# A two-layer AdaLN block (linear attention, RWKV and two FP4 feed-forwards) on one core: residual adds by an adding DMA, norm sums taken by ScalarE, a channel-mix key of half the matmuls, merged quantization halves, and feed-forward weights made ready inside the first turns

## What is computed

```python
h = layernorm(x) * (1 + ca) + sa
x = x + ga * attention(h)                      # x1, x3
h = layernorm(x) * (1 + cb) + sb
x = x + gb * ffn(h)                            # x2, x4
# ffn: gate, up = fp4(h) @ fp4(w_gate).T, fp4(h) @ fp4(w_up).T      (128 -> 352)
#      out = fp4(silu(gate) * up) @ fp4(w_down).T                   (352 -> 128)
# fp4(v): blocks of 16 along the last axis, scale = max|block| / 6, values rounded to 8 magnitudes
# layer 0: q, k, v, beta, mix = projections of h, rope on q and k, phi = elu + 1
#      K[t] = K[t-1]*beta + phi_k ; S[t] = S[t-1]*beta + phi_k v    (two decays m per head)
#      y = sum_m mix_m * (phi_q S) / (phi_q K) ; z = h + y @ Wout.T + bout ; layernorm(z) * g + b
# layer 1: RWKV: xn = layernorm(x) ; k, v, r = (xn mixed with the token before) @ weights
#      x = x + wkv(k, v) * sigmoid(r) @ w_output
#      xn2 = layernorm(x) ; key = (xn2*mix + shift(xn2)*(1-mix)) @ f_w_key    (128 -> 512)
#      x + sigmoid(receptance) * (relu(key)**2 @ f_w_value)
```

## Time and profile before

| what | value |
|---|---|
| median of 3 runs | 1495.9 us (1495.53 to 1497.5) |
| the profiled execution: its own time | 1494.11 us |
| its span, from the first to the last instruction | 1492.3 us |
| mean granted clock of TensorE, as a share of 2.4 GHz | 0.946 |
| busy: PE, DVE, ACT, POOL | 1290.4, 1202.6, 959.7, 191.6 us |
| x loaded, out stored | 16 DMAs each, 256 KB |

### The profile page before, as it was taken

How to read it: one execution, slowest core, us unless ns; L and a number is a source line. 1 busy time by engine, 2 the same in 40 slices (tenths; PEclk the granted TensorE clock), 3 DMA queues, 4 the chain that set the end, 5 groups by cost and what they waited for, 6 DMA issues and landing times.

```text
span 1492.3 us, 19655 instructions
## 1 busy us (share of the span) xinstructions
PE 1290.4 (86%) x5770; PEld 803.0 (54%) x5770; DVE 1202.6 (81%) x2423; ACT 959.7 (64%) x2145; POOL 191.6 (13%) x238
## 2 busy tenths in 40 slices
PE   1466898898989898989989898989989898989775
PEld 1233355555656565555656565655656565656453
DVE  6558677789898898979888898979888898986554
ACT  1434565758586767768585767768585767766664
POOL 1000202011111102021111102011110102020000
PEclk9968899999999999999999999999999999999897
DMA  3000000000000000000000000000000000000000
GB/s 117 0 8 1 7 1 1 8 1 8 8 8 8 8 1 15 1 16 0 7 7 7 9 0 14 0 15 0 7 7 7 9 0 14 0 7 1 8 7 14
DMA packets 21333, 13.45 MB, mean 9 GB/s; under 512 B 1396, under 2 KB 20472, under 8 KB 21240
## 3 DMA queue, kind: packets, MB, share of 16 engines
q1 hardware_dynamic: 12792, 8.29, 1.9%
q10 hardware_dynamic: 8448, 4.20, 1.0%
HBM read 8.28 MB, written 4.19 MB: 8 GB/s over the span
## 4 chain that ended last, share of the span: by engine, by line
PE 68%; ACT 11%; DVE 9%; issue 8%; POOL 2%; DMA 0%; ACTq 0%; DVEq 0%; SPq 0%; POOLq 0%
PE ps L1059 8%; PE ps L1155 6%; PE ps L852 4%; PE ps L964 4%; PE ps L1255 4%; PE ps L872 4%; PE ps L887 4%; PE ps L1246 3%; PE ps L1122 3%; PE ps L1247 3%; PE ps L960 2%; PE ps L926 2%; PE ps L898 2%; PE ps L1192 2%; PE ps L939 2%
## 5 line engine op out<-in xcount | busy, mean ns | idle before, releaser
L1059 PE MATMUL ps<-wguT,hqcol 128*128 128x352 f32 x512 | 174.5, 476 | 3.9 <-issue 3.9
L1500 DVE TENSOR_TENSOR_SCAN state<-beta,outer 128x512 f32<-128x512 f32 x128 | 149.2, 1207 | 0.0
L1059 PEld LDWEIGHTS ps<-wguT,hqcol 128*128 128x128 f32 x512 | 94.5, 197 | 63.0 <-issue 25.7
L401 POOL TENSOR_TENSOR rstd_of_a<-var_of_a,minus_half 128x4 f32<-128x4 f32 x32 | 39.1, 1222 | 625.0 <-DVE var_of_a L1460 625.0
L1360 DVE SCALAR_TENSOR_TENSOR hid<-hmag,hid 128x704 f32<-128x704 f32 x128 | 113.0, 883 | 2.0 <-ACT hmag L652 0.4
L1155 PE MATMUL ps<-hidcol,wdT 128*128 128x256 f32 (+1 forms) x384 | 94.8, 390 | 3.9 <-DVE outer L1491 2.0
L1577 DVE TENSOR_TENSOR hid<-th,ps 128x352 f32<-128x352 f32 x128 | 64.6, 515 | 26.9 <-ACT th L639 18.3
L1155 PEld LDWEIGHTS ps<-hidcol,wdT 128*128 128x128 f32 (+1 forms) x384 | 70.4, 193 | 26.7 <-DVE outer L1491 10.3
L639 ACT ACTIVATE th<-ps 128x352 f32<-128x352 f32 x128 | 59.6, 467 | 37.6 <-PE ps L1059 34.5
L1526 DVE TENSOR_TENSOR state<-state,qk 128x1024 f32<-128x1024 f32 x64 | 76.1, 1209 | 0.0
L660 ACT ACTIVATE hidcol<-ps 128x512 f32<-128x512 f32 x64 | 38.2, 597 | 57.7 <-PE ps L1122 57.0
(11 more groups left out here) (232 smaller groups left out, 3417.0 us busy)
## 6 DMA issues: line engine op xcount, KB each, us to landing
xin<-in_x SPq DMA_DIRECT2D x16, 256.0 KB, 2.8
out<-x ACTq DMA_DIRECT2D x16, 256.0 KB, 2.3
const<-in_const SPq DMA_DIRECT2D x1, 848.0 KB, 6.1
state<-in_wmod SPq DMA_DIRECT2D x1, 768.0 KB, 4.7
outer<-in_w_gate_up SPq DMA_DIRECT2D x2, 128.0 KB, 6.1
wqk<-in_wqk SPq DMA_DIRECT2D x1, 256.0 KB
key_mixed<-in_fw_key SPq DMA_DIRECT2D x1, 256.0 KB
fw_val<-in_fw_val SPq DMA_DIRECT2D x1, 256.0 KB
```

Source lines behind the costliest of these rows:

```text
L1059: t_.matmul(bank(f"f{l}_{'gu'[g]}{t}")[:, 0:I_FF], hqcol[l][:, t * P:(t + 1) * P], wguT[:, l, g, :], start=True, stop=True).then_inc(s_gu[ ...
L1500: return v.tensor_tensor_scan(state[:, m, c, :], beta[:, m, :], src, 0.0, ALU.mult, ALU.add)
```

## The change

**Residual adds.** x is loaded straight into the rows `xa`, where the sums x1 and x2 stay; x3 and x4 are in `xb`. For x1, x3 and x4 TensorE only transposes the gated term to rows (`rows_from`), ScalarE copies it to SBUF, and a DMA issued by GpSimd adds it to the rows in place (`accum_op=ALU.add`). Each of these DMAs stands behind a tiny `tensor_tensor` into `pool_scrap`. x2 stays on TensorE.

**Norm sums.** f0, a1 and f1 lose `bn_stats` and `bn_aggr`. ScalarE's copy out of PSUM is cut in four tiles that accumulate their row sums (`rows_out`), VectorE makes the mean with one small instruction (`mean_f0` and its like; for f0 and f1 it is the old rows' mean plus the added term's), ScalarE squares the deviations from SBUF in four tiles (`spread_squares`, after the DMA has landed), and GpSimd needs three small instructions (`power_of_spread`) where it had two.

**Mixed key.** ScalarE (`c5x`) and VectorE (`c5k`) mix the channel mix's input once, into `xk`, and four matmuls do the key where eight did.

**z matmuls.** The two halves over m are summed in PSUM (`a_n`), so `a6` has one set over `ycol`; `bout` is added by ScalarE to a copy of the columns (`a1b`, `hcolb`). `a5y` copies `a_n` out on ScalarE and `a5q` multiplies on VectorE.

**Merged halves.** `b4`, `b4q` and three steps of `c4` work on whole tiles: 1408 values a row in place of twice 704.

**Cut of the turns.** The turn is cut at another place: the ends of `a4` and `a5` of pair n - 1 stand at the top of turn n, `b1` of layer 1 is at n - 3 throughout, and the store is at n - 4.

**Weights.** The early loads are reordered (x of pair 0 third), and the quantization of the feed-forward weights is spread in 18 pieces a layer over VectorE's turns 0 and 1 (`weight_blocks`), their transposes too (`turn_weights`); `late_weights` makes the rest ready in turn 0.

The diff, cut to its core:

```diff
+        hmag = [hidcol[l].rearrange("p c t -> p (c t)")[:, 0:NT * I_FF] for l in range(2)]
...
+        def at_start(step, pair, *more):
+
+            if isinstance(pair, int) and pair == 0:
+                step(*more)
...
+            sp.dma_start(cT[:, :, :], a["cT"]).then_inc(s_cond, 16)
+            sp.dma_start(wmod[:, :, :], a["wmod"].rearrange("l p n -> p l n")).then_inc(s_wmod, 16)
+            sp.dma_start(of_pair(xa, 0), x_v[0, :, :, :]).then_inc(s_x[0], 16)
+            sp.dma_start(const[:, :], a["const"]).then_inc(s_const, 16)
+            for dst, src in ((wvT, "wv"), (wbmT, "wbm"), (vec[:, :], "vec"), (bbeta[:, :], "bbeta"), (bmix[:, 0:2], "bmix"),
+                             (wqk[:, :, :], "wqk"), (woutT[:, :], "wout")):
+                sp.dma_start(dst, a[src]).then_inc(s_load, 16)
+            sp.dma_start(bout[:, :], a["bout"].rearrange("o h -> h o")).then_inc(s_load, 16)
...
+            def power_of_spread(ln, i):
+                pool.wait_ge(s_squares[ln], i + 1)
+                before(pool, s_norm[ln], i, NT)
+                g.tensor_tensor(var[ln][:, :], squares[ln][:, :], eps_sum[:, :], ALU.add).then_inc(s_shift[ln], 1)
+                after(pool, s_shift[ln], i, 3, 1)
                 g.tensor_tensor(rstd[ln][:, :], var[ln][:, :], minus_half[:, :], ALU.pow).then_inc(s_shift[ln], 1)
-                after(pool, s_shift[ln], i, 2, 1)
-                g.tensor_tensor(shift[ln][:, :], negm[ln][:, :], rstd[ln][:, :], ALU.mult).then_inc(s_shift[ln], 1)
...
+            def add_x1(i):
+                pool.wait_ge(s_urow, i + 1)
+                g.tensor_tensor(pool_scrap[:, 0, :], minus_half[:, :], eps_tile[:, :], ALU.mult)
+                g.dma_start(of_pair(xa, i), urow[:, :, :], accum_op=ALU.add).then_inc(s_x1, 16)
...
             def body(n):
+                do(power_f0, n - 2)
+                do(power_c1, n - 3)
+                do(add_x4, n - 4)
+                do(add_x3, n - 3)
                 do(power_f1, n - 3)
-                do(power_f0, n - 1)
+                do(power_a1, n - 2)
+                do(power_b1, n - 2)
                 do(power_a0, n)
-                do(power_c1, n - 2)
-                do(power_a1, n - 1)
-                do(power_b1, n - 1)
-                do(power_z0, n)
+                do(power_z0, n - 1)
+                do(add_x1, n - 1)
             turns(pool, body)
 
...
+            def spread_squares(ln, i, rows, spare):
+                act.wait_ge(s_mean[ln], i + 1)
+                for t in range(NT):
+                    at = (i % 2) * NT + t
+                    ins = s.activation(spare[:, t, :], rows[:, at, :], ACT.Square, bias=negm[ln][:, at:at + 1],
+                                       accum_out=squares[ln][:, t:t + 1])
+                ins.then_inc(s_squares[ln], 1)
+
+            def rows_out(ln, i, name, dst, done):
+                before(act, s_mean[ln], i)
+                for t in range(NT):
+                    ins = s.activation(dst[:, t, :], tiles_of(name)(t), ACT.Copy, accum_out=sums[ln][:, t:t + 1])
+                ins.then_inc(done, 1)
+
+            def b1v(l, i):
+                before(act, s_fqT[l], i)
+                if l == 0:
+                    act.wait_ge(s_x1, 16 * i + 16)
+                else:
+                    act.wait_ge(s_x3, 16 * i + 16)
+                spread_squares(f"f{l}", i, (xa, xb)[l], hq[l])
+
+            def c1v(j):
...
-            def a5(i, q):
-                after(act, s_share_mm, i, SEQ, q + 1)
-                s.activation(share_c[:, :, q * T:(q + 1) * T], bank(f"a_s{q}").rearrange("p (m t) -> p m t", m=M), ACT.Copy)\
-                    .then_inc(s_share_c, 1)
+            def a5y(i):
+                after(act, s_num, i, 2 * M)
+                before(act, s_z, i)
+                s.activation(ycol[:, :], bank("a_n"), ACT.Copy).then_inc(s_yc, 1)
...
+            def c5x(j):
+                act.wait_ge(s_xs[1], j + 1)
+                before(act, s_fk_mm, j, 4)
+                s.activation(xk.rearrange("p (s t) -> p s t", s=SEQ), xs[1][:, :, 0:T], ACT.Identity, scale=omix[:, 3:4]).then_inc(s_xkp, 1)
...
-                    last = t_.matmul(bank(f"a_n{m}")[c * NH:(c + 1) * NH, :], cst("sel_num"), state[:, m, c, :], start=True, stop=True,
-                                     tile_position=(0, c * NH))
+                    last = t_.matmul(bank("a_n")[c * NH:(c + 1) * NH, :], cst("sel_num"), state[:, m, c, :], start=(m == 0),
+                                     stop=(m == M - 1), tile_position=(0, c * NH))
                 last.then_inc(s_num, 1)
...
-                t_.matmul(bank("a_z"), ones_row[:, :], bout.rearrange("p t h -> p (t h)"), start=True, stop=False)
...
-                    t_.matmul(dst, hcol[0][:, t * P:(t + 1) * P], center, start=False, stop=False)
-                    t_.matmul(dst, ycol[:, 0, t * P:(t + 1) * P], woutT[:, :], start=False, stop=False)
-                    last = t_.matmul(dst, ycol[:, 1, t * P:(t + 1) * P], woutT[:, :], start=False, stop=(t == NT - 1))
+                    t_.matmul(dst, hcolb[:, t * P:(t + 1) * P], center, start=True, stop=False)
+                    last = t_.matmul(dst, ycol[:, t * P:(t + 1) * P], woutT[:, :], start=False, stop=True)
...
-            def a8x(i):
-                pe.wait_ge(s_x, 16 * i + 16)
-                freed(pe, s_wexp_in, i - 1)
-                freed_at_ends(pe, s_outer, i, 2, 1)
-                rows_of(bank("a_x1"), xin)
...
+            def rows_from(dst, cols):
+                for t in range(NT):
+                    last = t_.transpose(dst[:, t * P:(t + 1) * P], cols[:, t * P:(t + 1) * P], ident)
+                return last
...
-                add_columns(bank("a_x1"), ucol).then_inc(s_x1mm, 1)
+                rows_from(bank("a_x1"), ucol).then_inc(s_urowT, 1)
...
-                dst = bank(f"c_f{c}").rearrange("p (s t) -> p s t", s=SEQ)
-                t_.matmul(dst, key_mixed[:, 0, c * P:(c + 1) * P], xs[1][:, :, 1:T + 1], start=True, stop=False)
-                t_.matmul(dst, key_mixed[:, 1, c * P:(c + 1) * P], xs[1][:, :, 0:T], start=False, stop=True).then_inc(s_fk_mm, 1)
+                t_.matmul(bank(f"c_f{c}"), fw_key[:, c * P:(c + 1) * P], xk[:, :], start=True, stop=True).then_inc(s_fk_mm, 1)
...
+            def mean_f0(i):
+                after(dve, s_lnc, i, 3)
+                dve.wait_ge(s_urow, i + 1)
+                before(dve, s_shift["f0"], i, 3)
+                v.scalar_tensor_tensor(of_pair(negm["f0"], i), sums["f0"][:, :], -1.0 / H, of_pair(negm["a0"], i), ALU.mult, ALU.add)\
+                    .then_inc(s_mean["f0"], 1)
...
+            def late_weights():
...
+            def a5q(i, q):
+                after(dve, s_share_mm, i, SEQ, q + 1)
+                after(dve, s_phi, i, 2)
+                toks = slice(q * T, (q + 1) * T)
+                v.tensor_tensor(qshare[:, :, toks], bank(f"a_s{q}").rearrange("p (m t) -> p m t", m=M),
+                                phi[:, 0:1, toks].to_broadcast([P, M, T]), ALU.mult).then_inc(s_qsh, 1)
...
+            def b4(l, i, part):
                 if part == 0:
-                    after(dve, s_hid[l], i, NT, 2 * k + 2)
-                else:
-                    after(dve, s_hch[l][k], i, 3, part)
-                scale_blocks(part, half(l, k), half(l, k), blk[l], k * HALF, HALF, 1 / 6.0, SCALE_MIN)\
-                    .then_inc(s_hn[l] if part == 3 else s_hch[l][k], 1)
-
-            def b4q(l, i, k, part):
+                    after(dve, s_hid[l], i, NT)
+                else:
+                    after(dve, s_hch[l], i, 5, part)
+                w = hid[l].rearrange("p t (b e) -> p (t b) e", e=BLK)
...
+            def c5k(j):
+                dve.wait_ge(s_xkp, j + 1)
+                v.scalar_tensor_tensor(seqs(xk[:, :]), xs[1][:, :, 1:T + 1], vec[:, 9:10], seqs(xk[:, :]), ALU.mult, ALU.add)\
+                    .then_inc(s_xk, 1)
...
-                do(layer(b4q, 1), n - 4, 0, 1)
+                at_start(gates, n)
+                at_start(weight_blocks, n, 0, 0, 0)
+                at_start(weight_blocks, n, 0, 0, 1)
...
+                do(a2p, n, 1)
+                at_start(late_weights, n)
+                do(a4dp, n)
+                do(layer(b4q, 0), n - 1, 0)
```

1244 lines of the change are left out of this document (637 added, 607 removed), and 10 rows, old and new, of the table BANK.

## The result

The changed kernel takes 1455.99 us (median of 4 runs, 1452.08 to 1457.94) where the kernel before takes 1495.72 on the same chip, a ratio of 0.973 with a 95% interval of 0.9705 to 0.9755. It is 2.7% faster. The profiled execution has a span of 1454.8 us and a mean granted clock of 0.899 of 2.4 GHz (before: 0.946).

What follows compares the result with a forecast made beforehand. TensorE was taken to lead, with VectorE close behind and stopping the gain, so the turn follows VectorE. Set-up 66.5 + 15 turns x 78.8 + tail 179 + 3.6 = 1431 us, range 1370 to 1497.

Steps and rivals of the forecast that it cites:

- Set-up: Stretch before the first z matmuls: from 91.6 to 66.5 us, bounds 58 to 75, with q and k near 18.
- layer 1's pieces: Quantizing layer 1's weights on VectorE in turn 1: 11.1 us, left out of the sum, +11 once if they show.
- TensorE's and VectorE's work: Busy time per turn: TensorE loses 9.3 us; VectorE loses 4.7, bounds 4.2 to 5.2.
- The turn: Interval between z matmuls: follows VectorE's -4.7 us, gives back one chain's 1.3, from 82.2 to 78.8 us.
- a longer norm chain: A norm's chain through ScalarE and GpSimd: copies, mean, squares and a third GpSimd instruction lengthen it by about 1.3 us.
- the tail: Stretch after the last z matmuls, where the last pair's chain has no cover: 166.9 + 12 = 179 us.
- TensorE's case: Rival that TensorE sets the turn, 17%: 1343 us, up to 1381 if half of the difference is lost.
- The DMAs: Adding DMAs on GpSimd's queue: land in 2.3 us plus 0.24 for the scrap instruction, hidden under ScalarE's other work.
- rule on the shared port: VectorE instructions with two SBUF inputs hinder GpSimd's SBUF reads and can starve its DMA descriptors; trace: 239 against 1571 ns.
- TensorE's work alone: Rival, 17%: the turn follows TensorE's 72.9 us, giving 1343 us in all.
- The set-up alone: Rival, 18%: turns stay at 82.2 us because the waits move with the new cut; only the set-up gains, 1482 us.
- The late DMA: Rival, 16%: hindered GpSimd makes x1's and x3's adds late, up to 6.4 us a turn; 1506 us, at most 1527.

Runs made afterwards that it cites:

- e2: Changed kernel with all 36 pieces of the feed-forward weights' quantization ahead of VectorE's first turn: 1470.44 us, ratio 0.9832.
- e12: Changed kernel with the norm sums undone for f0, a1 and f1 (bn_stats on VectorE, no squares on ScalarE): 1459.7 us, ratio 0.9759.
- e3: Changed kernel with each of the four key matmuls made twice on TensorE: 1506.41 us, ratio 1.0063.
- e1: Changed kernel with the adds of x1 and x3 back on TensorE instead of adding DMAs, x4 keeping its DMA: 1497.05 us, ratio 1.0.
- e7: Changed kernel with layer 0's four products on VectorE made once more into a scrap tile: 1479.08 us, ratio 0.9879.
- e11: Changed kernel with two more powers on GpSimd ahead of x1's adding DMA: 1490.17 us, ratio 0.994.
- e6: Changed kernel with norm a1 ahead of f1 on ScalarE, GpSimd and TensorE, and the last step of b4q in halves: 1473.85 us.
- e8: Changed kernel with a1's statistics by bn_stats and bn_aggr on VectorE again, without its squares on ScalarE: 1447.86 us, ratio 0.9674.
- e10: Changed kernel with a1's statistics by bn_stats again and f1's columns, rows, magnitudes and rounding moved earlier: 1477.14 us.

## Why the prediction was right, and where its sum was off

**Set-up.** q and k came at 20.25 us (18 expected) and the first z at 64.5 (66.5). Right in size. Not right was that layer 1's pieces would be free in turn 1: the text priced them at 11 if they showed and left them out, and e2 puts 9.8 us on the pieces of both layers in the first three intervals.

**TensorE's and VectorE's work.** -9.2 against -9.3 for TensorE, of which 0.9 is the lower clock behind the jump (-8.5 from a turn without it), and -3.6 against -4.7 for VectorE. e12 puts 3.5 us of VectorE's work on the norms, where the sum had 3.9; for all the rest this leaves 0.1, where the sum had 0.8. ScalarE +6.2 against +7. GpSimd's 16.5 for 11.7 had no term.

**The turn.** I let it follow VectorE and gave back 1.3 for a longer norm chain: -3.4 from the average of 82.2. In the loop it fell by 3.5, from 83.7 to 80.2. This agreement is luck. By the neighbouring turns, 2.0 of the 3.5 are the wait behind the loop's jump, which the sum does not know; against a turn without it the fall is 1.5, made of VectorE's -3.6 and of 2.0 us more idle time on VectorE. What the term had right is that a longer wait on VectorE takes back a part of the work it is spared. But e3, e1 and e7 show that neither engine sets the turn alone, for work added to either goes through whole. And the stretch of a1's chain between x2's copies and its norm grew by 4.5 us, not by 1.3; what the sum left out or priced too low were f1's squares, which stand ahead of a1's, and the powers beside VectorE's products, 2.09 and 1.84 us for 1.0.

**The step that failed** is the line "82.2 - 4.7 + 1.3 = 78.8" for all 15 intervals; measured they average 80.6. It carries one average through three kinds of turn. The first three intervals did not fall but rose by 12.4 us, of which e2 puts 9.8 on the weights' pieces. The other twelve fell by 36.4 us, of which some 16 are the four waits behind the jump that are gone, and 1.7 a turn the rest. In all that is -24 us against -51. The set-up was 2.0 us shorter than summed and the tail 1.6 longer (180.6 against 179), and the median lies 1.2 us above the span and not 3.6; together these make the 25 us between 1431 and 1456. One bound of a rival is also off: TensorE's case with half of the 5.9 us a turn lost comes to 1387, not 1381.

**The DMAs.** Landing 3.3 us against 2.3, scrap instructions 0.2 to 0.5 us (one of 1.4), both hidden as expected. The 2.6 us that the prediction estimates from the Trainium skill ("DMA: Bandwidth & Descriptors", "Anatomy of one DMA — SWDGE (gpsimd) path") was nearer, and still short. The Trainium skill's rule on the shared port ("SBUF — State Buffer", "Who interferes with whom") is borne out for GpSimd's small instructions by 2.09 against 1.01 us for the same power on four columns; the DMAs' issue, 0.86 to 0.92 us each with one of 1.05, shows no such hold in this case.

**The rivals.** TensorE's work alone (1343) is out: 5.7 of its 9.2 us turned into waiting. The set-up alone (1482) is out: the 15 intervals gave 24 us, 8 even without the four jumps. The late DMA is out, since ScalarE never waits for one in the loop; e11 shows its price.

**What stays open.** Undoing the adds costs 41 us and doubling the key's matmuls 50, far more than the 40 that the whole change gained together, so something in it gave back some 5.7 us of waiting on TensorE in each turn. 3.7 of them are the longer wait for f1's rows, which is still 3.1 us a turn when the squares are gone (e12). No run brought the idle time back, for TensorE's is between 10.9 and 12.8 us in every one. Not undone in any run are the new cut of the turns, the mixing of the key's input ahead of its matmuls, the z matmuls over summed halves, and the merged quantization (e6 has only its last step in halves and moved nothing). Which of these it is was not tried.

## What to carry to other kernels

In a software pipeline whose engines are 80 to 86% busy and wait for each other in order, idle time is not slack: here 3.8 us of TensorE work, 1.5 of VectorE work or 1.3 of a late DMA lengthened the turn by as much or more, while the idle time of the engine in question stayed the same or grew. To price a change in such a kernel, cut the unrolled turns, the loop and the tail apart, look inside the loop for turns that the jump lengthens, and do not carry an average over all. Moving a sum of squares to an engine with idle time gains nothing when it stands on a norm's chain (e12), and moving an add to a DMA gained at least the matmuls' whole time here, where the DMA has cover (e1).

## What the runs showed of the hardware

- GpSimd's 128x4 power took 1.0 us alone and 1.8 to 2.1 beside VectorE's products of two SBUF tiles.
- After waits of 4 to 5 us TensorE's next matmuls ran at the lower of its two levels (granted clock 0.50 to 0.54; 3.30 us for what took 1.91 at 1.00). When a DMA came 1.3 us late in e11, the turn grew by 2.4 us, of which 1.4 is TensorE's busy time.
- A DMA of 256 KB that adds in place, issued by GpSimd, landed in 3.3 us; a plain store on ScalarE's queue took 2.3.
- Once in each round of the hardware loop, ahead of the first instruction behind the jump back, VectorE stands still for 1.9 to 2.0 us and ScalarE for 2.1 in the kernel before, and VectorE for 1.4 to 1.8 in e8, e10 and e12, with nothing in the profile that releases them. The changed kernel has no such wait. Before, the turn behind the jump was 3.9 us longer than its neighbour.
